# Second matmul of the first MLP: fp32 products replaced by three fp32r products of split halves

## The chip, the cores and the metric

The kernel runs on one core of a Trainium2 chip. The metric is the device time of one execution in microseconds. The kernel before took 510.92 us (median of three runs, 509.15 to 511.65). The core has five engines that run their own instruction queues in program order and meet at semaphores: TensorE (PE, matrix products into PSUM banks), VectorE (DVE), ScalarE (ACT), GpSimd (POOL, no access to PSUM) and SyncE (SP, which issues the DMAs).

## The reference, cut to what matters

One transformer layer on x of shape 8 x 512 x 256. First a block with causal linear attention and an MLP with exact gelu, then a second MLP with ternary weights and a layer norm between its matmuls. The change touches the line marked below.

```python
def attn_block(x, ...):                      # called with _layernorm(x)
    x_norm = _layer_norm(x, ln1_w, ln1_b)
    Q = elu(_linear(x_norm, q_w, q_b)) + 1.0
    K = elu(_linear(x_norm, k_w, k_b)) + 1.0
    V = _linear(x_norm, v_w, v_b)
    attn = _linear(_causal_linear_attn(Q, K, V), o_w, o_b)
    x = x + attn
    h = _layer_norm(x, ln2_w, ln2_b)
    h = gelu(_linear(h, f1_w, f1_b), approximate=False)    # 256 -> 1024
    x = x + _linear(h, f2_w, f2_b)                         # 1024 -> 256: the change
    return x

def ffn(x, ...):                             # called with _layernorm(x)
    h = gelu(x @ absmean(W_fc).T, approximate=False)       # weights -1, 0, 1
    h = layernorm(h, ln_w, ln_b)
    return h @ absmean(W_proj).T
```

## The kernel before, in words

The eight batch elements (g = 0 to 7, 512 rows of 256) are worked one after another, in a software pipeline. `step(g)` holds the first MLP, the second MLP's first half of batch element g, the attention of g + 1, and what is left of g - 1. Each engine has its own lists of calls, `first()`, `step(g)` for g = 1 to 5, and `last()`; the order of the calls in a list is the order of the engine's instructions. There is no scheduler; semaphores alone tie the lists together, and each call begins with the waits it needs.

Precision is kept by splitting. A matrix product in fp32 is either issued as it is, or its operands are cut into a high part (a copy into fp32r, on ACT, the `_hi` calls) and a low part (value less high part, on DVE, the `_lo` calls through `lo_part`, L795), and `split3` (L175 to L179) adds three products in the same bank: high by high, high by low, low by high. Before the change all large products but one went this way. The exception is the second matmul of the first MLP.

The first MLP runs over eight tiles m of 128 hidden columns. `f1(g, m)` writes 128 x 512 into `bank_f[m % 2]` (six products of 512 columns, L177 to L179), `gelu(g, m)` (L581, ACT) reads the bank and writes one tile of `hring`, a ring of `RH` = 8 tiles in SBUF, and `f2(g, k)` (L347) multiplies that tile, as 4 x 128 rows, by `wf2[:, k, :]` and adds it into the two banks `bank_y`: four fp32 products of 128 x 256. f1(m) waits for gelu(m - 2) to free its bank. When f2 is through all eight, `y_sum` (L872, DVE) adds the banks to the residual, a layer norm follows (statistics on DVE, the power on POOL, L1006, the shift on DVE, L773, the scaling on ACT, `z3_norm`), PE flips the result through `bank_f` (`tz3`, L185), and `fc` (L366) starts the second MLP. `tr` (L380) and `proj` (L396), with `g_hi` (L612) and `g_lo` (L912), are its second half; `tu`, `qk_mm`, `scores`, `v_mm`, `attend` and `tz2` belong to attention.

At the start the kernel loads weights and prepares them while batch element 0 goes through attention: `wf1_hi` and `wf1_lo` split the first matmul's weights, `abs_part` (L483) sums the absolute values of the ternary weights, `ternary` (L736, L738) makes them. Small staging tensors (`wqk_raw`, `wv_raw`, `wo_raw`, `wide`, the row selectors) live in the tiles of `hring`, which is not in use yet. On POOL `n1o` (L1024) and `xpb` (L1035) add rows to the residuals.

Of the kernel before, what the change touches and what calls it, by code (L numbers as in the profile page):

```python
# [19 lines left out]
def build(nc, x, wqk_d, wv_d, wo_d, f1_d, f2_d, fc_d, pj_d, vec_d, rows_d, out):  # L20
# [14 lines left out]
    with ExitStack() as ctx:  # L35
# [138 lines left out]
        def _(pe):  # L174
# [227 lines left out]
            def first():  # L402
# [7 lines left out]
                tr(0, 0, 1); tz2(1, 0); fc(0, 3, 0); fc(0, 3, 1); tr(0, 0, 2); proj(0, 0, 0); tr(0, 0, 3)  # L410
                proj(0, 0, 1); tz2(1, 1); tr(0, 1, 0); proj(0, 0, 2); proj(0, 0, 3)

            def step(g):

                f1(g, 0); tr(g - 1, 1, 1); f1(g, 1); tr(g - 1, 1, 2); tu(g + 1, 0); f1(g, 2); f1(g, 3); f1(g, 4)
                tu(g + 1, 1); f1(g, 5); proj(g - 1, 1, 0); tr(g - 1, 1, 3); qk_mm(g + 1); f1(g, 6); f2(g, 0)
                f1(g, 7); f2(g, 1); f2(g, 2); f2(g, 3); scores(g + 1); f2(g, 4); f2(g, 5); f2(g, 6); f2(g, 7)
                v_mm(g + 1, 0); v_mm(g + 1, 1); proj(g - 1, 1, 1); proj(g - 1, 1, 2); proj(g - 1, 1, 3); tz3(g, 0)
                attend(g + 1, 0); attend(g + 1, 1); attend(g + 1, 2); tz3(g, 1); fc(g, 0, 0); attend(g + 1, 3)
                fc(g, 0, 1); fc(g, 1, 0); fc(g, 1, 1); tr(g, 0, 0); tr(g, 0, 1); fc(g, 2, 0); fc(g, 2, 1)  # L420
                tr(g, 0, 2); fc(g, 3, 0); tr(g, 0, 3); proj(g, 0, 0); fc(g, 3, 1); tz2(g + 1, 0); tz2(g + 1, 1)
                proj(g, 0, 1); proj(g, 0, 2); tr(g, 1, 0); proj(g, 0, 3)
# [697 lines left out]
```

## Time and profile before

| | us |
|---|---|
| median of three runs | 510.92 |
| the profiled execution | 510.98 |
| its span | 509.3 |
| PE busy | 479.6 (94%) |
| DVE busy | 349.3 (69%) |
| ACT busy | 289.0 (57%) |
| POOL busy | 129.7 (25%) |
| PE, products of `f2` (L347) | 114.7, 512 records |

The span is the time from the first to the last instruction. Busy is the union of an engine's instructions; PE's ends are modelled, and products overlap in the records, so the pace of products is read from their starts. An idle time is followed by the engine that ended it. In the second fence the granted clock (PEclk) is a share of full speed.

### The profile page before, as it was taken

What the parts mean: (1) busy time and instruction counts of PE and PEld (TensorE: products, weight loads), DVE (VectorE), ACT (ScalarE), POOL (GpSimd) and SP (SyncE); (2) the same over time, 40 slices, a digit from 0 to 9 for tenths busy, and PEclk for the clock granted to TensorE, in tenths of its full rate; (3) what the DMA queues carried; (4) which work ended last, traced back from release to release, by engine and by line L of the source; (5) the groups of instructions that cost most, each with busy time, mean ns of one, the idle gap of its engine ahead of it and who ended that gap; (6) DMA issues with size and microseconds to landing.
All of it is one profiled execution on the core that took longest, in us unless ns stands there. A gap on an engine that the chain in (4) does not pass through costs nothing.

```text
span 509.3 us, 8086 instructions
## 1 busy us (share of the span) xinstructions
PE 479.6 (94%) x2802; PEld 421.8 (83%) x2802; DVE 349.3 (69%) x931; ACT 289.0 (57%) x543; POOL 129.7 (25%) x128
## 2 busy tenths in 40 slices
PE   5786998999999999999999999999999999999796
PEld 4784887888989888888988888888988889888686
DVE  4688528695589638876589639876589638954467
ACT  3654664773557645774557745774559733752263
POOL 2134104220163005420163005420163004302210
PEclk9765999999999999999999999999999999999989
DMA  7230000100010000100010000100010000000001
GB/s 263 99 125 1 1 0 1 42 22 1 1 64 1 21 1 21 44 21 1 1 62 2 22 0 22 42 23 1 0 63 2 21 2 21 2 22 0 22 1 42
DMA packets 10040, 14.03 MB, mean 28 GB/s; under 512 B 784, under 2 KB 9104, under 8 KB 9488
## 3 DMA queue, kind: packets, MB, share of 16 engines
q1 hardware_dynamic: 10000, 13.52, 7.7%
q8 instruction: 22, 0.36, 0.3%
q14 instruction: 18, 0.15, 0.1%
HBM read 9.32 MB, written 4.19 MB: 27 GB/s over the span
## 4 chain that ended last, share of the span: by engine, by line
PE 40%; issue 33%; DVE 10%; POOL 9%; ACT 4%; DMA 2%; SPq 0%; POOLq 0%; DVEq 0%; ACTq 0%
PE bank_y L347 8%; PE bank_f L366 7%; PE bank_p L396 5%; PE bank_f L177 4%; PE bank_f L178 3%; PE bank_f L179 3%; PE bank_y L380 3%; POOL rs L1006 3%; PE bank_a L185 2%; DVE sh L773 2%; DMA out<-yc 2%; POOL y L1042 1%; POOL xa L1024 1%; POOL yc L1052 1%; DVE bn L877 1%
## 5 line engine op out<-in xcount | busy, mean ns | idle before, releaser
L347 PE MATMUL bank_y<-wf,hring 128*128 128x256 f32 x512 | 114.7, 379 | 0.0
L1006 POOL TENSOR_TENSOR rs<-ve,neg_half 128x2 f32<-128x2 f32 x48 | 33.7, 703 | 310.0 <-DVE ve L768 310.0
L347 PEld LDWEIGHTS bank_y<-wf,hring 128*128 128x128 f32 x512 | 96.7, 190 | 13.5
L912 DVE SCALAR_TENSOR_TENSOR g_lo<-bank_y,vec,g_hi 128x256 fp32r<-128x256 f32 x128 | 55.1, 476 | 22.3 <-ACT g_hi L612 22.1
L396 PE MATMUL bank_p<-wpj_t,g_hi 128*128 128x256 f32 x256 | 64.6, 289 | 0.7 <-DVE yc L921 0.7
L581 ACT ACTIVATE hring<-bank_f,f_bias 128x512 f32<-128x512 f32 x64 | 43.2, 686 | 35.1 <-PE bank_f L179 34.5
L396 PE MATMUL bank_p<-wpj_t,g_lo 128*128 128x256 f32 x256 | 62.0, 280 | 0.0
L612 ACT ACTIVATE g_hi<-bank_y,vec 128x256 fp32r<-128x256 f32 x128 | 52.8, 484 | 11.8 <-PE bank_y L380 11.6
L177 PE MATMUL bank_f<-z2T_hi,wf_hi 128*128 128x512 f32 x128 | 55.2, 431 | 1.4 <-DVE z2T_lo L795 1.4
L366 PE MATMUL bank_f<-wfc_t,z3T_hi 128*128 128x512 f32 x128 | 54.3, 424 | 0.9 <-DVE z3T_lo L795 0.9
L603 ACT ACTIVATE h<-bank_f 128x512 f32<-128x512 f32 x64 | 38.7, 604 | 24.1 <-PE bank_f L366 23.9
L178 PE MATMUL bank_f<-z2T_lo,wf_hi 128*128 128x512 f32 x128 | 51.5, 402 | 0.0
L179 PE MATMUL bank_f<-z2T_hi,wf_lo 128*128 128x512 f32 x128 | 51.3, 401 | 0.0
L366 PE MATMUL bank_f<-wfc_t,z3T_lo 128*128 128x512 f32 x128 | 51.2, 400 | 0.0
L396 PEld LDWEIGHTS bank_p<-wpj_t,g_hi 128*128 128x128 f32 x256 | 48.1, 188 | 1.3 <-issue 0.9
L396 PEld LDWEIGHTS bank_p<-wpj_t,g_lo 128*128 128x128 f32 x256 | 48.2, 188 | 0.2
L892 DVE BATCH_NORM_STATS2 bn<-h 128x6 f32<-128x512 f32 x64 | 41.1, 682 | 3.1 <-ACT h L603 2.9
L380 PE MATMUL bank_y<-ident,h 128*128 128x128 f32 x256 | 37.4, 272 | 0.7 <-ACT h L603 0.7
L380 PEld LDWEIGHTS bank_y<-ident,h 128*128 128x128 f32 x256 | 30.7, 141 | 6.1 <-ACT h L603 1.1
L500 ACT ACTIVATE z<-y,sh,rs 128x256 f32<-128x256 f32 x32 | 17.5, 595 | 28.8 <-DVE sh L773 28.8
L773 DVE SCALAR_TENSOR_TENSOR sh<-mv,rs 128x2 f32<-128x2 f32 x48 | 30.4, 634 | 4.0 <-POOL rs L1006 3.5
L366 PEld LDWEIGHTS bank_f<-wfc_t,z3T_hi 128*128 128x128 f32 x128 | 24.6, 192 | 7.8 <-issue 2.3
(156 smaller groups left out, 991.5 us busy)
## 6 DMA issues: line engine op xcount, KB each, us to landing
x_sb<-in_x SPq DMA_DIRECT2D x16, 256.0 KB, 2.8
out<-yc SPq DMA_DIRECT2D x16, 256.0 KB, 2.1
h<-in_f SPq DMA_DIRECT2D x1, 1024.0 KB, 7.6
wf<-in_f SPq DMA_DIRECT2D x1, 1024.0 KB, 9.6
h<-in_fc SPq DMA_DIRECT2D x1, 1024.0 KB, 11.6
h<-in_pj SPq DMA_DIRECT2D x1, 1024.0 KB, 4.9
hring<-in_wv SPq DMA_DIRECT2D x1, 256.0 KB, 3.5
hring<-in_wo SPq DMA_DIRECT2D x1, 256.0 KB, 3.6
```

Source lines behind the costliest of these rows:

```text
L177: pe.matmul(ps, w[0], r[0], start=start, stop=False, skip_group_check=skip)
L178: pe.matmul(ps, w[0], r[1], start=False, stop=False, skip_group_check=skip)
L179: return pe.matmul(ps, w[1], r[0], start=False, stop=stop, skip_group_check=skip)
L347: mm = pe.matmul(bank_y[t // 2][:, (t % 2) * D:(t % 2 + 1) * D], hring[:, (8 * g + k) % RH, t * P:(t + 1) * P], wf2[:, k, :], start=(k == ...
L366: mm = pe.matmul(bank_f[c][:], z3T[part][:, k, t * P:(t + 1) * P], wfc[:, k, c * 512:(c + 1) * 512], start=(k == 0 and part == 0), stop=(k ...
L380: mm = pe.transpose(bank_y[q % 2][:, (2 * i + t) * P:(2 * i + t + 1) * P], h3[:, 2 * h + t, m * P:(m + 1) * P], ident[:])
L396: mm = pe.matmul(bank_p[:, t * D:(t + 1) * D], gr[part][:, (8 * g + 4 * h + q) % RG, i, t * P:(t + 1) * P], wpj[:, m, :], start=(m == 0 an ...
L581: act.activation(hring[:, (8 * g + m) % RH, :], bank_f[m % 2][:], ACT.Gelu, bias=f1_bias[:, m:m + 1]).then_inc(s["h_ready"], 1)
L612: act.activation(gr[0][:, n % RG, i, :], bank_y[q % 2][:, i * D:(i + 1) * D], ACT.Copy, scale=ln3w_c[:, m:m + 1]).then_inc(s["g_hi"], 1)
L892: dve.bn_stats(bn[3][:, t, 6 * c:6 * c + 6], h3[:, t, c * 512:(c + 1) * 512]).then_inc(s["ln4_bn"], 1)
L912: dve.scalar_tensor_tensor(gr[1][:, n % RG, i, :], bank_y[q % 2][:, i * D:(i + 1) * D], ln3w_c[:, m:m + 1], gr[0][:, n % RG, i, :].bitcast ...
L1006: pool.tensor_tensor(rs[n][:, 2 * h:2 * h + 2], ve[n][:, 2 * h:2 * h + 2], neg_half[:, 0:2], ALU.pow).then_inc(s[f"ln{n + 1}_rs"], 1)
```

## The change

- The weights of the second matmul are kept as `wf2_hi` and `wf2_lo` (fp32r). Four ACT copies and four POOL subtractions make them at the start, from raw weights that are loaded into the memory of `y` and `yc`, now one tensor `y_yc`.
- `gelu` writes its result back into `bank_f`. A new ACT call `h_hi` copies the bank into `h_hi`, a new DVE call `h_lo` subtracts that from the bank into `h_lo`. Both are rings of four tiles (`RH` = 4), in place of one ring of eight.
- `f2` calls `split3`: twelve fp32r products of 128 x 256 a tile in place of four fp32 ones. f1(m) and the flips `tz3` now wait for h_lo, not for gelu.
- The staging tensors move from `hring` to `qk_relu`, `z`, `xa` and a small tensor `few_rows`; for this `n1(0)`, `qk_max(0)`, `abs_part(0)` and `xpb(0)` get a wait each.
- The lists of calls of PE, ACT, DVE and POOL are written in another order, in `first`, `step` and `last`.

```diff
-RH = 8
+RH = 4
-        wf2 = sb("wf2", [P, KH, D])
+        wf2 = [sb("wf2_hi", [P, KH, D], F32R), sb("wf2_lo", [P, KH, D], F32R)]
-        hring = sb("hring", [P, RH, N])
+        hr = [sb("h_hi", [P, RH, N], F32R), sb("h_lo", [P, RH, N], F32R)]
...
             def f1(g, m):
...
                 if m >= 2:
-                    pe.wait_ge(s["h_ready"], 8 * g + m - 1)
+                    pe.wait_ge(s["h_lo"], 8 * g + m - 1)
...
             def f2(g, k):
...
-                        pe.wait_ge(s["f2_loaded"], 16)
+                        pe.wait_ge(s["wf2_lo"], 4)
...
-                pe.wait_ge(s["h_ready"], 8 * g + k + 1)
+                pe.wait_ge(s["h_lo"], 8 * g + k + 1)
                 for t in range(T):
-                    mm = pe.matmul(bank_y[t // 2][:, (t % 2) * D:(t % 2 + 1) * D],
-                                   hring[:, (8 * g + k) % RH, t * P:(t + 1) * P], wf2[:, k, :],
-                                   start=(k == 0 and t % 2 == 0), stop=(k == KH - 1), skip_group_check=True)
+                    mm = split3(bank_y[t // 2][:, (t % 2) * D:(t % 2 + 1) * D],
+                                [r[:, (8 * g + k) % RH, t * P:(t + 1) * P] for r in hr], [w[:, k, :] for w in wf2],
+                                k == 0 and t % 2 == 0, k == KH - 1, skip=True)
...
+            def wf2_hi(n):
+                act.wait_ge(s["f2_loaded"], 16)
+                act.activation(wf2[0][:, 2 * n:2 * n + 2, :], f2_raw[:, 2 * n:2 * n + 2, :], ACT.Copy).then_inc(s["wf2_hi"], 1)
...
             def gelu(g, m):
                 act.wait_ge(s["f1_done"], 8 * g + m + 1)
...
+                act.activation(bank_f[m % 2][:], bank_f[m % 2][:], ACT.Gelu, bias=f1_bias[:, m:m + 1]).then_inc(s["h_gelu"], 1)
+
+            def h_hi(g, m):
+                act.wait_ge(s["h_gelu"], 8 * g + m + 1)
                 if 8 * g + m >= RH:
                     act.wait_ge(s["f2_done"], 8 * g + m - RH + 1)
...
+                act.activation(hr[0][:, (8 * g + m) % RH, :], bank_f[m % 2][:], ACT.Copy).then_inc(s["h_hi"], 1)
...
+            def h_lo(g, m):
+                dve.wait_ge(s["h_hi"], 8 * g + m + 1)
+                lo_part(hr[1][:, (8 * g + m) % RH, :], bank_f[m % 2][:], hr[0][:, (8 * g + m) % RH, :], "h_lo")
...
+            def wf2_lo(n):
+                pool.wait_ge(s["wf2_hi"], n + 1)
+                pool.tensor_tensor(wf2[1][:, 2 * n:2 * n + 2, :], f2_raw[:, 2 * n:2 * n + 2, :],
+                                   wf2[0][:, 2 * n:2 * n + 2, :].bitcast(F32), ALU.subtract).then_inc(s["wf2_lo"], 1)
...
PE, def step(g):
-                f1(g, 0); tr(g - 1, 1, 1); f1(g, 1); tr(g - 1, 1, 2); tu(g + 1, 0); f1(g, 2); f1(g, 3); f1(g, 4)
...
+                proj(g - 1, 0, 2); f1(g, 0); f1(g, 1); tu(g + 1, 0); tr(g - 1, 1, 1); proj(g - 1, 0, 3)
+                tr(g - 1, 1, 2); f1(g, 2); proj(g - 1, 1, 0); tr(g - 1, 1, 3); f1(g, 3); f1(g, 4); f2(g, 0)
+                tu(g + 1, 1); f2(g, 1); f1(g, 5); qk_mm(g + 1); f2(g, 2); f1(g, 6); f1(g, 7); f2(g, 3); f2(g, 4)
...
```

On PE, in a middle step, this is the place where the first tile of the second matmul stands. Before, it comes after f1(g, 6), with the last f1 behind it:

```order
L177 MATMUL bank_f<-z2T_hi,wf_hi 128x512
L178 MATMUL bank_f<-z2T_lo,wf_hi 128x512
L179 MATMUL bank_f<-z2T_hi,wf_lo 128x512
L347 MATMUL bank_y<-wf,hring 128x256 x4
L177 MATMUL bank_f<-z2T_hi,wf_hi 128x512
L178 MATMUL bank_f<-z2T_lo,wf_hi 128x512
L179 MATMUL bank_f<-z2T_hi,wf_lo 128x512
```

Now the third tile, f2(g, 2), stands behind the attention's query and key product (`bank_a`); of its twelve products three rows are shown, and f1(g, 6) follows them:

```order
L178 MATMUL bank_a<-uT_hi,wqk_hi 128x512
L179 MATMUL bank_a<-uT_lo,wqk_hi 128x512
L180 MATMUL bank_a<-uT_hi,wqk_lo 128x512
L178 MATMUL bank_y<-wf_hi,h_hi 128x256
L179 MATMUL bank_y<-wf_lo,h_hi 128x256
L180 MATMUL bank_y<-wf_hi,h_lo 128x256
```

The tiles of f2 thus begin right after f1(g, 4) and stand between the later f1; the last five, f2(g, 3) to f2(g, 7), come in one piece, before the scores and not around them.

On DVE, at the start of a middle step (`yc<-bank_p` is `output`, `uT_lo` the split for attention, `qk_relu` the first call behind qk_mm), before:

```order
L904 SCALAR_TENSOR_TENSOR yc<-pj_rows_b,sh,yc 128x256 x2
L921 SCALAR_TENSOR_TENSOR yc<-bank_p,rs,yc 128x256 x2
L795 TENSOR_TENSOR uT_lo<-bank_a,uT_hi 128x2x256
L912 SCALAR_TENSOR_TENSOR g_lo<-bank_y,vec,g_hi 128x256 x2
L795 TENSOR_TENSOR uT_lo<-bank_a,uT_hi 128x2x256
L912 SCALAR_TENSOR_TENSOR g_lo<-bank_y,vec,g_hi 128x256 x4
L806 TENSOR_SCALAR qk_relu<-bank_a,qk_bias 128x512
L892 BN_STATS bn<-h 128x6 x2
```

The same place now:

```order
L933 SCALAR_TENSOR_TENSOR g_lo<-bank_y,vec,g_hi 128x256 x4
L811 TENSOR_TENSOR h_lo<-bank_f,h_hi 128x512
L942 SCALAR_TENSOR_TENSOR y_yc<-bank_p,rs,y_yc 128x256 x2
L933 SCALAR_TENSOR_TENSOR g_lo<-bank_y,vec,g_hi 128x256 x2
L811 TENSOR_TENSOR h_lo<-bank_f,h_hi 128x512
L933 SCALAR_TENSOR_TENSOR g_lo<-bank_y,vec,g_hi 128x256 x2
L811 TENSOR_TENSOR h_lo<-bank_f,h_hi 128x512
L933 SCALAR_TENSOR_TENSOR g_lo<-bank_y,vec,g_hi 128x256 x2
L811 TENSOR_TENSOR h_lo<-bank_f,h_hi 128x512
L811 TENSOR_TENSOR uT_lo<-bank_a,uT_hi 128x2x256
L811 TENSOR_TENSOR h_lo<-bank_f,h_hi 128x512
L811 TENSOR_TENSOR uT_lo<-bank_a,uT_hi 128x2x256
```

The low halves of the new tiles stand one by one between the g_lo of the batch element before, and the two u_lo have moved behind them.

## Rows read from the trace of the kernel before

**Rows 1.** The page's head: span, then busy time of the engines.
```profile
span 509.3 us, 8086 instructions
...
PE 479.6 (94%) x2802; PEld 421.8 (83%) x2802; DVE 349.3 (69%) x931; ACT 289.0 (57%) x543; POOL 129.7 (25%) x128
```
**Rows 2.** Busy by stretch: length, busy (count) of each engine, granted clock, DMA.
```profile
0.00:46.00 46.00, 30.68 (x150) 27.26 (x151) 30.14 (x87) 26.11 (x48) 12.63 (x17) 0.79 0.38 135
...
218.30:275.70 57.40, 56.70 (x344) 50.31 (x344) 41.06 (x112) 34.56 (x66) 15.89 (x15) 1.00 0.06 19
...
460.00:509.30 49.30, 41.10 (x236) 35.55 (x234) 28.71 (x73) 16.32 (x33) 8.46 (x9) 0.95 0.05 17
```
**Rows 3.** Waits of PE from 218.3 to 275.7: in total, times, longest.
```profile
PE bank_f L185 <- ACT z L500: 0.7, 1, 0.7
```
**Rows 4.** Timeline of PE, 230 to 300: start, length, line, out<-in, count.
```profile
243.01 7.07 PE L347 MATMUL bank_y<-wf,hring 128*128 128x256 f32 x32
...
250.03 0.28 PE L178 MATMUL bank_a<-wvo_lo,uT_hi 128*128 128x256 f32 x1
...
252.79 0.28 PE L396 MATMUL bank_p<-wpj_t,g_hi 128*128 128x256 f32 x1
...
255.50 0.28 PE L396 MATMUL bank_p<-wpj_t,g_lo 128*128 128x256 f32 x1
...
276.15 0.39 PE L177 MATMUL bank_f<-z2T_hi,wf_hi 128*128 128x512 f32 x1
...
277.55 0.60 PE L380 MATMUL bank_y<-ident,h 128*128 128x128 f32 x4
```
**Rows 5.** Groups by line and shape: count, busy us, mean ns, idle before.
```profile
L347 PE MATMUL bank_y<-wf,hring 128*128 128x256 f32 x512 | 114.7, 379 | 0.0
...
L581 ACT ACTIVATE hring<-bank_f,f_bias 128x512 f32<-128x512 f32 x64 | 43.2, 686 | 35.1 <-PE bank_f L179 34.5
...
L396 PEld LDWEIGHTS bank_p<-wpj_t,g_hi 128*128 128x128 f32 x256 | 48.1, 188 | 1.3 <-issue 0.9 <-DVE g_lo L912 0.2
...
L795 DVE TENSOR_TENSOR z2T_lo<-bank_a,z2T_hi 128x512 fp32r<-128x512 f32 x16 | 10.9, 689 | 2.3 <-ACT z2T_hi L571 2.3
...
L571 ACT ACTIVATE z2T_hi<-bank_a 128x512 fp32r<-128x512 f32 x16 | 9.5, 596 | 2.9 <-PE bank_a L185 2.9
...
L526 ACT ACTIVATE bank_a<-bank_a,qk_bias 128x512 f32<-128x512 f32 x8 | 5.3, 662 | 2.3 <-DVE qk_relu L806 2.3
```
**Rows 6.** Timeline of ACT, 230 to 300; idle before in brackets.
```profile
243.21 0.38 ACT L552 ACTIVATE af_hi<-bank_a 128x256 fp32r<-128x256 f32 x1 [4.65 <-PE bank_a L274]
...
279.57 0.69 ACT L581 ACTIVATE hring<-bank_f,f_bias 128x512 f32<-128x512 f32 x1 [1.13 <-PE bank_f L179]
280.16 1.56 ACT L612 ACTIVATE g_hi<-bank_y,vec 128x256 fp32r<-128x256 f32 x4
```
**Rows 7.** Timeline of DVE, 230 to 300.
```profile
246.69 0.69 DVE L795 TENSOR_TENSOR ae_lo<-bank_a,ae_hi 128x512 fp32r<-128x512 f32 x1 [6.49 <-ACT ae_hi L546]
```
**Rows 8.** Timeline of PE in the start.
```profile
27.73 0.58 PE L177 MATMUL bank_a<-wvo_hi,uT_hi 128*128 128x256 f32 x1 [1.37 <-DVE ae_lo L795]
...
45.32 0.80 PE L177 MATMUL bank_f<-z2T_hi,wf_hi 128*128 128x512 f32 x1 [1.41 <-DVE z2T_lo L795]
...
50.61 0.39 PE L177 MATMUL bank_f<-z2T_hi,wf_hi 128*128 128x512 f32 x1
```
**Rows 9.** Timeline of POOL in the start.
```profile
26.30 2.95 POOL L1035 TENSOR_TENSOR y<-x_sb,rows_b 128x512 f32<-128x512 f32 x2
37.76 0.71 POOL L1006 TENSOR_TENSOR rs<-ve,neg_half 128x2 f32<-128x2 f32 x1 [8.51 <-DVE ve L768]
```
**Rows 10.** Timeline of DVE in the start.
```profile
22.77 4.11 DVE L711 SCALAR_TENSOR_TENSOR wf_lo<-h,vec,wf_hi 128x512 fp32r<-128x512 f32 x3
...
49.67 0.74 DVE L736 TENSOR_SCALAR yc<-h,theta 128x1024 f32<-128x1024 f32 x1
50.45 1.28 DVE L738 SCALAR_TENSOR_TENSOR wfc_t<-h,theta,yc 128x1024 fp32r<-128x1024 f32 x1
```

More of the change, by code:

```diff
@@ L413, in step @@
+                tz2(1, 0); fc(0, 2, 1); fc(0, 3, 0); proj(0, 0, 0); tr(0, 0, 2); tz2(1, 1); fc(0, 3, 1); tr(0, 0, 3)
+                proj(0, 0, 1); tr(0, 1, 0)
             def step(g):
[L415 to L417 removed]
@@ L418, in step @@
[L418 to L422, printed above, removed]
@@ new lines, in first @@
+                qk_exp(0); wf1_hi(2); qk_hi(0); n1(0); wf1_hi(3); wf2_hi(0); ae_hi(0); af_hi(0); wf2_hi(1); ad_hi(0)
+                wf2_hi(2); eps_split(); v_hi(0, 0); wf2_hi(3); v_hi(0, 1); abs_part(0); abs_part(1); ln3_hi()
+                abs_part(2); abs_part(3); z2_norm(0, 0); z2_norm(0, 1); z2_hi(0, 0); z2_hi(0, 1); u_norm(1, 0)
+                gelu(0, 0); h_hi(0, 0); u_hi(1, 0); gelu(0, 1); h_hi(0, 1); u_norm(1, 1); gelu(0, 2); u_hi(1, 1)
+                h_hi(0, 2); gelu(0, 3); n1(1); h_hi(0, 3); qk_exp(1); gelu(0, 4); h_hi(0, 4); rows(); qk_hi(1)
@@ new lines, in first @@
+                gelu(0, 5); h_hi(0, 5); gelu(0, 6); h_hi(0, 6); ae_hi(1); af_hi(1); ad_hi(1); gelu(0, 7); h_hi(0, 7)
+                spread_copy(); v_hi(1, 0); v_hi(1, 1); z3_norm(0, 0); z3_hi(0, 0); z3_norm(0, 1); z3_hi(0, 1)
+                gelu3(0, 0, 0); gelu3(0, 0, 1); gelu3(0, 1, 0); z2_norm(1, 0); g_hi(0, 0, 0); gelu3(0, 1, 1)
+                gelu3(0, 2, 0); z2_norm(1, 1); g_hi(0, 0, 1); z2_hi(1, 0); gelu3(0, 2, 1); g_hi(0, 0, 2)
+                z2_hi(1, 1); gelu3(0, 3, 0); g_hi(0, 0, 3); gelu3(0, 3, 1); u_norm(2, 0)
@@ L931, in first @@
-                ln2_shift(0, 1); threshold(); z2_lo(0, 0); z2_lo(0, 1); ln1_stats(1); ternary(0); ln1_shift(1)
-                ternary(1); ternary(2); u_lo(1, 0); ternary(3); u_lo(1, 1); qk_max(1); qk_sum(1); qk_lo(1)
-                ad_mask(1); ad_lo(1); ae_lo(1); af_lo(1); y_sum(0, 0); ln3_stats(0, 0); y_sum(0, 1); v_lo(1, 0)
-                ln3_shift(0, 0); v_lo(1, 1); ln3_stats(0, 1); attn_out(1, 0); ln3_shift(0, 1); attn_out(1, 1)
-                ln2_stats(1, 0); attn_out(1, 2); z3_lo(0, 0); z3_lo(0, 1); ln2_stats(1, 1); attn_out(1, 3)
@@ new lines, in first @@
+                consts(); ln1_stats(0); selectors(); ln1_shift(0); wide_cols(); wqk_lo(); u_lo(0, 0); u_lo(0, 1)
+                qk_bias_add(); qk_max(0); bo_rows(); wvo_lo(); qk_sum(0); wf1_lo(0); wf1_lo(1); f1_bias_add()
+                qk_lo(0); wf1_lo(2); ad_mask(0); ae_lo(0); af_lo(0); ad_lo(0); wf1_lo(3); eps_lo(); v_lo(0, 0)
+                v_lo(0, 1); attn_out(0, 0); attn_out(0, 1); ln2_stats(0, 0); attn_out(0, 2); ln2_stats(0, 1)
+                ln2_stats(0, 2); ln2_var(0, 0); attn_out(0, 3); ln2_stats(0, 3); ln2_var(0, 1); ln2_shift(0, 0)
@@ new lines, in first @@
+                ln2_shift(0, 1); ln1_stats(1); z2_lo(0, 0); z2_lo(0, 1); threshold(); ln1_shift(1); ln3_lo()
+                ternary(0); h_lo(0, 0); ternary(1); h_lo(0, 1); u_lo(1, 0); u_lo(1, 1); h_lo(0, 2); ternary(2)
+                qk_max(1); h_lo(0, 3); ternary(3); qk_sum(1); h_lo(0, 4); qk_lo(1); h_lo(0, 5); ad_mask(1); af_lo(1)
+                h_lo(0, 6); h_lo(0, 7); ad_lo(1); ae_lo(1); y_sum(0, 0); ln3_stats(0, 0); y_sum(0, 1); v_lo(1, 0)
+                ln3_shift(0, 0); v_lo(1, 1); ln3_stats(0, 1); attn_out(1, 0); ln3_shift(0, 1); ln2_stats(1, 0)
```

204 lines of the change are left out of this document (102 added, 102 removed).

## The prediction

> **What bounds the kernel now.** I read the page's head first: TensorE (PE) is busy 479.6 of 509.3 us, VectorE (DVE) 69%, ScalarE (ACT) 57% [rows 1]. A mean over stages says little, so next the busy time by stretch [rows 2]. In a middle step (57.4 us, one batch element's MLPs and the next one's attention) PE is busy 56.7 us, DVE 41.1, ACT 34.6. PE idles for 15 us in the first 46 us and for 8 in the last 49. In the middle step the table of waits names one wait of PE, 0.7 us, for the normalised input of the second MLP [rows 3]. So from about 46 to 460 us the time is the sum of what PE is given, and a microsecond taken off PE there is one off the span, as long as DVE and ACT keep up.
>
> The clock was granted at 1.00 in the middle stretches (the 2.4 GHz level), 0.79 in the start [rows 2].
>
> **The products themselves: 19.2 us less.** A tile of the second matmul (`f2`) is four products of 256 columns. In fp32 each leaves two MATMUL records: 64 tiles, 512 records [rows 5]. Their pace is read from start to start, since the durations overlap (a record is 379 ns long): from 243.01, where four tiles begin, to 250.03, where the second product of the next group begins, lie 7.02 us [rows 4]. One fp32r product (0.12, below) is in them, so 32 records take 6.90, 0.216 each. A tile costs 8 x 0.216 = 1.73 us. The new tile is 12 one-record products of 256 columns in fp32r. The kernel has just such work: from 250.03 to 252.79 the value projection runs 23 of them in 2.76 us, 0.120 each, and the last projection 23 in 2.71 from 252.79 to 255.50, 0.118 each [rows 4]. Both load new weights for every product, as the new tile does. I take 0.119: 12 x 0.119 = 1.43 us. Saved: 0.30 us a tile, 64 tiles, 19.2 us (0.118 and 0.120 give 20.1 and 18.6). All tiles lie in stretches where PE is saturated.
>
> A rule that speaks against this is in the Trainium skill, page "TensorE: Matmul & The Clock Gate", section "Part 3: Packing small matmuls": a weight load overlaps matmuls in flight only when it goes to another row group. The trace disagrees here: with loads of 188 ns in front of every product [rows 5] the pace stays 0.119 [rows 4]. I return to it as a rival.
>
> **What ACT and DVE get.** ACT's gelu writes into its bank: the nearest row is the in-place exponential, 662 ns, against 686 for today's gelu into SBUF [rows 5]. Added per tile: one ACT copy bank to fp32r, 0.60 (596 ns), and one DVE subtraction, 0.69 (689 ns) [rows 5]. Per step that is 8 x 0.60 - 8 x 0.02 = 4.6 us on ACT, making 39, and 5.5 us on DVE, making 46.6, in a step of about 54.3: neither is the bound. They also fall in the right half: today in the f1/f2 stage DVE stands idle for 6.49 us and ACT for 4.65 in single waits [rows 6, 7]. No table load comes in between: the `g_hi` copies begin at 280.16, while the gelu of 279.57 (0.69 long) is just ending [rows 6].
>
> **The new waits.** Each bank_f half is now held for gelu, copy and subtraction: 0.66 + 0.60 + 0.69 plus some 0.1 of hops = 2.05 us from the end of f1(m), before f1(m+2) may write it; today 0.7. What PE has queued in between, by the new order, in prices of 1.40 for an f1 (276.15 to 277.55), 0.44 for four transposes (0.60 less 0.16 by which an end is modelled late) [rows 4], 1.43 for an f2 and 0.95 for a proj (8 x 0.119): behind f1(0) 3.7 us, f1(1) 5.0, f1(2) 2.8 (proj, tr, f1(3)), f1(3) 4.7, f1(4) 7.5, f1(5) 4.2. The tightest, f1(2) to f1(4), has 0.75 to spare. Twice something stands in the chain: the two `u_norm` (about 1.1) between gelu(3) and h_hi(3) make 3.1 of 4.7; `qk_max` (about 0.7), which waits for qk_mm, ahead of h_lo(5) makes 3.0 of 4.2. Queued behind a late h_lo on DVE are the g_lo of the batch before and u_lo, for which PE's tr, proj and qk_mm wait. output(g-1,0) stands ahead of h_lo(g,1) and waits for proj(g-1,0,3), which is why that proj is issued before f1(g,2): 2.4 us are left there. The ring of four asks only that f2(m-4) is done before h_hi(m); by the new order f2(3) ends before gelu(7) can start. Unforeseen stalls are bounded by 0 and, by the larger of the two chain links (0.69) once per step in 7 steps, 5 us; I take 0.5, near zero since every slack found is above 0.7.
>
> The 0.7 us wait in front of the second z flip [rows 3] stands in five middle steps. Behind the last f2 PE has 6.2 us of work ahead of the first flip (scores, two proj, v_mm, proj) where it had 5.7, and 2.8 instead of 2.9 between the flips. Bounds: nothing, and all 3.3 us gone; I take 1.6.
>
> **The start.** DVE now does two wf1_lo (1.37 each [rows 10]) and the bias before qk_lo, so scores(0) begins about 1.0 us later; but ae_lo no longer stands behind three wf1_lo, so v_mm(0), today at 27.73 [rows 8], moves by about 0.5 only. On POOL four wf2_lo (nearest row 1.5 each, the adds of that shape [rows 9]) come before xpb(0); the last waits for an ACT copy at about 32, so xpb(0) ends near 36.5, and ln2_rstd(0,0) is wanted at 37.76 [rows 9]: hidden, by 1.2 us. The four ACT copies (0.7 each) fill waits. wqk_hi behind u_norm(0) is hidden too: its low part is first read by qk_mm(0). Start: +0.5, bounds -0.5 and +2. In the first batch element the four ternary() (0.74 + 1.28 = 2.0 each on DVE [rows 10]) alternate with h_lo; f1(0,2) then waits for a subtraction that ends near 50.8 where it started at 50.61 today [rows 8]. +0.8, bounds 0 and +3.
>
> **Sum**, against the profiled execution's own 510.98 (span 509.3 and 1.7 around it; the median of the three runs is 510.92, the same): 510.98 - 19.2 - 1.6 + 0.5 + 0.5 + 0.8 = 492.0 us.
>
> **Rivals.**
> *The helpers bind in part.* h_lo comes late behind another DVE instruction in some tiles, PE stays the bound in the rest. For it: both queues are in order, every f1 now waits on two engines. Against it: 16 us of DVE idle per step today, 5.5 used. At 0.12 us a tile (7.7 us) the time is 500.
> *The chain replaces the saving (the slower side).* If the bank hand-over exposes one whole subtraction, 0.69 us, on every tile because h_lo always queues behind a g_lo that waits for ACT, 64 x 0.69 = 44 us are added: 536. The point from which it decides is 0.30 us a tile (2.4 us a step): beyond it the change loses. Against it: the slacks above are all larger than 0.7.
> *Weight loads show.* If the four more loads of a tile (12 for 8) were not hidden, 4 x 0.19 = 0.75 us a tile, 48 us: 540. Against it: the pace in rows 4. This is what the Trainium skill's rule on weight loads ("TensorE: Matmul & The Clock Gate", "Part 3") would make of it.
> *The start swallows it.* If wf2_lo delayed the z2 chain, at most 4 x 1.5 = 6 us: 498. Against it: the 1.2 us of slack.
>
> **Chances.** Forecast case 0.78 (own range 488 to 496), helpers in part 0.10, start 0.03, chain 0.07, weight loads 0.02. Low end: 510.98 - 20.1 - 3.3 - 0.5 + 0 = 487. High end: +2 and +3 at the start and 5 of stalls above 491.8 give 500, about which the partial rival lies; above it is left some 0.15. So 487.5 to 500. Half a per cent (2.6 us) is about what a measurement of this kernel can tell. Faster needs under 508.4: forecast, partial and start rival, 0.91, less a little for a chain that costs about what is gained: 0.90; same 0.03; slower 0.07.
>
> **What would show it.** In the changed trace: L178 to L180 writing bank_y, 768 records at 0.119 from start to start (wrong at 0.15 or more: the saving is gone at 0.144); a middle step of 54.3 to 54.7 us with PE idle under 1; waits of PE on DVE's h_lo under 0.5 us a step; DVE near 46.5 and ACT near 39 us a step; f1(0,0) within 1 us of today's 45.32 [rows 8]. The prediction is wrong if PE's waits on h_lo add up to more than 5 us, or PE's records are not faster.

## The result, and the profile after

The changed kernel takes 489.36 us (median of 4 runs, 487.23 to 490.18), the kernel before in the same comparison 510.13 (4 runs, 509.15 to 511.65): ratio 0.959, 95% interval 0.955 to 0.963. The forecast was 492.0, range 487.5 to 500. The profiled execution took 487.23, of which 485.5 are the span. Two executions further down lay far outside their fellows and are left out of every median here: one of 573.11 us (gelu in SBUF, new order) and the profiled one of 2513.73 us in experiment 4, so that the version with two more subtractions has no usable trace.

The page's head after, against [rows 1]: TensorE (PE) is busy for less time, the three helpers (DVE, ACT, POOL) for more.

```profile
span 485.5 us, 8738 instructions
...
PE 455.8 (94%) x3058; PEld 413.8 (85%) x3058; DVE 379.1 (78%) x995; ACT 326.1 (67%) x611; POOL 135.3 (28%) x132
```

The start, a middle step (f1(4,0) to f1(5,0)) and the end by stretch, against [rows 2]: length, busy (count) of PE, PEld, DVE, ACT, POOL, granted clock, DMA.

```profile
0.00:43.60 43.60, 27.16 (x148) 24.26 (x148) 29.12 (x91) 26.58 (x51) 19.18 (x22) 0.85 0.41 142
...
207.47:261.42 53.95, 53.93 (x376) 49.68 (x375) 44.33 (x119) 39.08 (x74) 15.96 (x16) 1.00 0.06 21
460.00:485.50 25.50, 21.49 (x130) 18.30 (x128) 17.86 (x46) 11.78 (x25) 1.79 (x3) 0.90 0.06 21
```

PE idles 0.02 us of 53.95: PE's work fills the middle step, and the step is 3.5 us shorter.

Groups by line and shape, against [rows 5]: the new products, one of the three groups of their weight loads, the subtraction, the gelu and the copy.

```profile
L178 PE MATMUL bank_y<-wf_hi,h_hi 128*128 128x256 f32 x256 | 72.1, 282 | 1.0 <-DVE h_lo L811 1.0
L179 PE MATMUL bank_y<-wf_lo,h_hi 128*128 128x256 f32 x256 | 71.5, 279 | 0.0
L180 PE MATMUL bank_y<-wf_hi,h_lo 128*128 128x256 f32 x256 | 71.4, 279 | 0.0
...
L180 PEld LDWEIGHTS bank_y<-wf_hi,h_lo 128*128 128x128 f32 x256 | 48.0, 187 | 0.0
...
L811 DVE TENSOR_TENSOR h_lo<-bank_f,h_hi 128x512 fp32r<-128x512 f32 x64 | 43.9, 688 | 28.3 <-ACT h_hi L593 27.5
L587 ACT ACTIVATE bank_f<-bank_f,f_bias 128x512 f32<-128x512 f32 x64 | 42.2, 660 | 13.9 <-PE bank_f L180 12.3
L593 ACT ACTIVATE h_hi<-bank_f 128x512 fp32r<-128x512 f32 x64 | 38.1, 597 | 3.3 <-PE bank_y L180 1.7
```

768 records, as foreseen, and in all of them only 1.0 us of waiting. A record's 280 ns is a duration; the pace is read from start to start. Timeline of PE in a dense stretch, first and last row shown (columns: start, length, line, out<-in, count):

```profile
232.10 0.28 PE L180 MATMUL bank_y<-wf_hi,h_lo 128*128 128x256 f32 x1
...
235.28 0.28 PE L180 MATMUL bank_y<-wf_hi,h_lo 128*128 128x256 f32 x1
```

27 products lie between the two starts: 3.18 / 27 = 0.118 us each, the pace of [rows 4].

Where the time went, from the starts of f1(g,0) in both traces: start -1.7 us; the first two steps together -5.9 (the new order moves two `proj` from the first into the second, so they are taken together); four middle steps -3.54 each, -14.2; from f1(6,0) to the end -2.0. Together -23.8; by medians -20.8, since the execution profiled after was the fastest of its four and the one profiled before lay 0.85 above the median of its four.

### The profile page after: what moved, and what is told of

Read it like the earlier page. It is cut to its first block, busy times and chain, and to the rows that moved or that the text cites. A ratio compares the mean times of both kernels' runs of the same rounds, so it can differ in the third digit from the quotient of the medians.

```text
span 485.5 us, 8738 instructions
## 1 busy us (share of the span) xinstructions
PE 455.8 (94%) x3058; PEld 413.8 (85%) x3058; DVE 379.1 (78%) x995; ACT 326.1 (67%) x611; POOL 135.3 (28%) x132
## 4 chain that ended last, share of the span: by engine, by line
PE 69%; DVE 12%; issue 10%; POOL 3%; ACT 3%; DMA 0%; DVEq 0%; POOLq 0%; ACTq 0%
PE bank_f L367 9%; PE bank_p L397 9%; PE bank_y L178 6%; PE bank_y L179 5%; PE bank_y L180 5%; PE bank_f L178 5%; PE bank_f L179 5%; PE bank_f L180 5%; PE bank_y L381 4%; PE bank_a L178 3%; PE bank_a L180 3%; PE bank_a L179 3%; PE bank_a L186 2%; DVE sh L789 2%; DVE g_lo L933 2%
## 5 line engine op out<-in xcount | busy, mean ns | idle before, releaser
L178 PE MATMUL bank_y<-wf_hi,h_hi 128*128 128x256 f32 x256 | 72.1, 282 | 1.0 <-DVE h_lo L811 1.0
L179 PE MATMUL bank_y<-wf_lo,h_hi 128*128 128x256 f32 x256 | 71.5, 279 | 0.0
L180 PE MATMUL bank_y<-wf_hi,h_lo 128*128 128x256 f32 x256 | 71.4, 279 | 0.0
L811 DVE TENSOR_TENSOR h_lo<-bank_f,h_hi 128x512 fp32r<-128x512 f32 x64 | 43.9, 688 | 28.3 <-ACT h_hi L593 27.5
L178 PE MATMUL bank_f<-z2T_hi,wf_hi 128*128 128x512 f32 x128 | 52.7, 412 | 1.4 <-DVE z2T_lo L811 1.4
L587 ACT ACTIVATE bank_f<-bank_f,f_bias 128x512 f32<-128x512 f32 x64 | 42.2, 660 | 13.9 <-PE bank_f L180 12.3
L180 PE MATMUL bank_f<-z2T_hi,wf_lo 128*128 128x512 f32 x128 | 51.1, 399 | 0.0
L178 PEld LDWEIGHTS bank_y<-wf_hi,h_hi 128*128 128x128 f32 x256 | 48.1, 188 | 2.7 <-DVE h_lo L811 1.2
L179 PEld LDWEIGHTS bank_y<-wf_lo,h_hi 128*128 128x128 f32 x256 | 48.0, 188 | 1.1
L180 PEld LDWEIGHTS bank_y<-wf_hi,h_lo 128*128 128x128 f32 x256 | 48.0, 187 | 0.0
L1054 POOL TENSOR_TENSOR xa<-xa,bo_b 128x512 f32<-128x512 f32 x16 | 21.4, 1359 | 93.0 <-ACT xa L507 93.0
```

Of the source, the lines that this page charges most:

```text
L178: pe.matmul(ps, w[0], r[0], start=start, stop=False, skip_group_check=skip)
L179: pe.matmul(ps, w[0], r[1], start=False, stop=False, skip_group_check=skip)
L180: return pe.matmul(ps, w[1], r[0], start=False, stop=stop, skip_group_check=skip)
L587: act.activation(bank_f[m % 2][:], bank_f[m % 2][:], ACT.Gelu, bias=f1_bias[:, m:m + 1]).then_inc(s["h_gelu"], 1)
L811: dve.tensor_tensor(dst, b, hi.bitcast(F32), ALU.subtract).then_inc(s[ready], 1)
L1054: pool.tensor_tensor(half(xa, h), half(xa, h), wide_row(bo_b[:]), ALU.add).then_inc(s["n1o_ready"], 1)
```

## The experiments

The kernel before ran beside each group on the same chip (medians 510.73, 511.07, 510.09). The changed kernel was rerun only in the first group (experiments 1, 2 and 3, and the two waits of 8); where a version of another group is set against its 488.31, the difference is one between chips, on which the kernel before differs by up to 1.0 us. "Step" below is the distance between two middle f1(g,0): 57.4 us before, 53.9 after.

**1. The changed kernel again**, to tell its own spread from effects.

> The changed kernel once more, unaltered, as the measure for the runs beside it. The profiled execution of it took 487.2 us while the others took 488.7 to 490.2, so this also tells which is typical. Expected: 489.4, plus or minus 1.5. Theory 'start': f1(0, 0) begins at 43.6 us again, 1.7 before the kernel before, because wf1_lo on DVE no longer runs beside POOL's adds. Rival 'luck': the start was a chance of one execution and f1(0, 0) lies anywhere between 43.6 and 46.

Measured: 488.31 (5 runs, 487.51 to 489.53), ratio 0.956 (0.954 to 0.958). Steps are the same to 0.02 us. f1(0,0) stood at 45.0, not 43.6, so most of the 1.7 us that the first trace shows at the start was chance; over nine traces of kernels in the new order it stood at 43.6 to 45.6, mean 44.5. In the one trace of before it stood at 45.3, and in the three other traces with the old lists (experiments 5 and 7) at 44.5 to 45.0. A gain at the start is therefore not shown.

**2. fp32 products in the new order**: the tables of the change, with the old second matmul, weights and ring, and no halves.

```diff
-    mm = split3(bank_y[...], [r[:, (8 * g + k) % RH, ...] for r in hr], [w[:, k, :] for w in wf2], ...)
+    mm = pe.matmul(bank_y[...], hring[:, (8 * g + k) % RH, ...], wf2[:, k, :], ...)
...
-    act.activation(bank_f[m % 2][:], bank_f[m % 2][:], ACT.Gelu, ...)
+    act.activation(hring[:, (8 * g + m) % RH, :], bank_f[m % 2][:], ACT.Gelu, ...)
```

> The new lists of calls and the moved staging memory, but the second matmul as before: fp32 products, gelu straight into a ring of eight, no copy, no subtraction, no split of its weights. Theory 'products': what is left of the change is the order and the start, worth 1.7 us at the start and about 0.7 us a middle step of waits, so 510.1 - 1.7 - 3.5 = 505, and the products account for 64 x (1.72 - 1.43) = 18.6 of the rest less the helpers' share. Rival 'order': the new order carries much of the gain, and this kernel comes in under 500.

Measured: 508.02 (506.96 to 508.23), ratio 0.994 (0.992 to 0.996), step 56.4. That is 3 us above the 505 expected, which had counted the 1.7 us of the start as real, and far above the rival's 500. So the order, with the moved staging memory, is worth 2.7 us alone, and products with their helpers 508.02 - 488.31 = 19.7 us (19.2 forecast), 2.5 a step. PE waits for `z` at the z flips: before 7.6 us in 9 places, here 4.1 in 3.

```profile
PE bank_f L186 <- ACT z L504: 4.1, 3, 2.2
PE bank_y L381 <- DVE g_lo L928: 3.7, 4, 1.7
```

The second row is new with the order, not with the halves: two of its waits are 1.63 and 1.66 us long. The middle step from f1(3,0) to f1(4,0), in the columns of [rows 2]:

```profile
216.50:272.90 56.40, 56.37 (x344) 50.45 (x343) 39.24 (x111) 34.74 (x66) 15.90 (x16) 1.00 0.06 20
```

DVE is busy 39.2 us of it, where it was 41.1 before: the new order alone takes 1.9 us off DVE.

**3. Two products in place of three** (the weights' low half left out of the second matmul).

```diff
-    mm = split3(...)          # hi*hi, hi*lo, lo*hi
+    pe.matmul(ps, hr[0][...], wf2[0][:, k, :], ...)
+    mm = pe.matmul(ps, hr[1][...], wf2[0][:, k, :], ...)
```

> The changed kernel with the product of the high half of h and the low half of wf2 left out, so two products in place of three; all copies and subtractions stay. 256 products of 0.119 us go, 30.5 us of PE. Theory 'PE is the only bound, with slack beside it': the time falls by 25 to 30 us, to 460 to 464, with a middle step of 50.1. Rival 'the helpers are just behind PE': DVE at 44.7 and ACT at 39.4 us of a 53.9 us step, and the hand-over of a bank (2.05 us) against only 2.8 us of PE work, let PE wait; the time falls by less than 15 us.

Measured: 473.7 (471.0 to 475.98, two executions near each end), ratio 0.927 (0.922 to 0.932), step 51.9. 256 products at 0.119 are 30.5 us; 14.6 came, and 2.0 of 3.8 in a middle step. The expected 460 to 464 was missed and the rival came out: the helpers are just behind PE. PE's waits:

```profile
PE bank_y L349 <- DVE h_lo L813: 10.8, 7, 2.8
```

In each middle step this is one wait of 1.5 us, before the last tile of the second matmul. Timeline of ACT before it (idle in brackets):

```profile
220.72 1.28 ACT L589 ACT_TABLE_LOAD   x1
222.01 0.66 ACT L589 ACTIVATE bank_f<-bank_f,f_bias 128x512 f32<-128x512 f32 x1
222.71 0.60 ACT L595 ACTIVATE h_hi<-bank_f 128x512 fp32r<-128x512 f32 x1
223.20 0.58 ACT L543 ACTIVATE q_stack<-bank_a 64x512 fp32r<-64x512 f32 x1
...
225.74 0.60 ACT L595 ACTIVATE h_hi<-bank_f 128x512 fp32r<-128x512 f32 x1
```

ACT runs nearly without a gap through a table load (`ACT_TABLE_LOAD`, 1.28 us, here back to gelu after the exponential) and the q and k copies, and h_hi of the last tile ends at 226.3. The changed kernel is therefore close to the end of this lever: with 3.8 us less work on PE in a step, the helpers already take half of it back.

**4. One and two more subtractions on DVE ahead of each h_lo.**

```diff
     dve.wait_ge(s["h_hi"], 8 * g + m + 1)
+    dve.tensor_tensor(spare[:, 0, ...], bank_f[m % 2][:], hr[0][...].bitcast(F32), ALU.subtract)
     lo_part(hr[1][...], bank_f[m % 2][:], hr[0][...], "h_lo")
```

> The changed kernel with one more DVE subtraction over 128 x 512 ahead of each h_lo, out of the same two tiles into spare memory (0.69 us each by h_lo's own row, 64 of them: 44 us of DVE in all). Theory (TensorE is the bound of a step, the wait for h_lo has slack, my bank chain's was 2.05 us): in a middle step DVE's work goes from 44.7 to 50.2 of 53.9 us and stays under it; the last row of products of a tile comes after h_lo by at least 0.7 us nearly everywhere, so the five middle steps stay at 53.9 to 54.4 and the whole kernel loses 0 to 3 us (most of it in the tail, where DVE ends the pass): 488 to 491. Rival (chain: f1 - gelu - h_hi - h_lo - f2 binds, no slack): each tile pays its 0.69 us, steps of 59.4 and a kernel of 525 to 532.

> The same with two more subtractions (1.38 us per tile). Theory: DVE's work in a middle step comes to 44.7 + 11.0 = 55.7 us, more than the 53.9 us of TensorE, so DVE becomes the bound: a middle step takes at least 55.8, with TensorE's waits for DVE some 2 to 5 us a step, and the kernel 500 to 520. If the slack were only that of the average (DVE free to run ahead), steps would be 55.7 to 56.5 (kernel 500 to 506); if the slack of the single tile (2.05 us) is the limit too, the waits in the dense stretch of f2 come on top (kernel 506 to 520). Rival (no slack at all): 64 times 1.38, a kernel of 570 or more.

Measured: with one 499.43 (498.49 to 500.34), ratio 0.978 (0.975 to 0.981); with two 520.7 (three executions, 519.3 to 520.9). A middle step with one:

```profile
265.22:319.71 54.49, 54.16 (x376) 49.55 (x375) 48.80 (x127) 38.99 (x74) 15.93 (x16) 1.00 0.07 20
```

Its waits of PE have two rows of this kind, f2 for its tile and f1 for its bank:

```profile
PE bank_y L179 <- DVE h_lo L812: 2.8, 1, 2.8
...
PE bank_f L179 <- DVE h_lo L812: 2.1, 6, 0.5
```

Eight subtractions more (DVE busy 48.8 us where it was 44.3) cost 0.6 us there, a little over the 0.5 that the forecast allowed: the slack of a middle step is real and holds most of one subtraction, but not all. In each of the five middle steps f1(g,4) now waits 0.3 us for the h_lo that frees its bank; this is the link that the prediction called the tightest. The kernel lost 11.1 us, not 0 to 3, since the two steps at the ends hold no slack (against the repeat of experiment 1 the step from f1(6,0) is 4.2 us longer, of which the first row, a wait for h_lo(6,7), is the most; the tail 2.4; the first two steps 1.9; the four middle ones together 2.3). With two subtractions the loss is 32.4 us, just above the 506 to 520 that the bound by DVE's sum and the single tile's slack gave.

**5. The halves in the old order** (the tables of before, each h_lo placed by hand, ring of eight), then **the same with gelu in SBUF**, so that the bank is free after gelu; and **gelu in SBUF in the new order**.

```diff
-    f1(g, 0); f1(g, 1); tu(g + 1, 0); tr(g - 1, 1, 1); proj(g - 1, 0, 3); tr(g - 1, 1, 2); f1(g, 2)
+    f1(g, 0); tr(g - 1, 1, 1); f1(g, 1); tr(g - 1, 1, 2); tu(g + 1, 0); f1(g, 2); f1(g, 3); f1(g, 4)
... and, in the two with gelu in SBUF:
-    pe.wait_ge(s["h_lo"], 8 * g + m - 1)      # f1: bank free
+    pe.wait_ge(s["h_gelu"], 8 * g + m - 1)
-    act.activation(bank_f[m % 2][:], bank_f[m % 2][:], ACT.Gelu, ...)
+    act.activation(hf[:, (8 * g + m) % 3, :], bank_f[m % 2][:], ACT.Gelu, ...)
```

> The changed products, gelu and halves, in the order of the kernel before on every engine: each high half follows its gelu at once, each h_lo stands on DVE among the old entries just ahead of where f2 needs it, the ring has eight tiles. It asks how much of the gain needs the new order. Theory: the order alone was worth 1.0 us a step with fp32 products; with halves the old order also puts two f2 close behind their f1 (f1(g,6), f2(g,0), f1(g,7), f2(g,1) to f2(g,7)), and the work of DVE and ACT around them was placed for a kernel without halves, so I expect TensorE to wait 0.5 to 2 us a step for h_lo or gelu and for what the halves delay: middle steps of 55.0 to 56.5, kernel 496 to 506. Rival (the order matters little, products carry all): steps of 54.5 to 54.9, kernel 491 to 494. Other rival (helpers unplaced eat the gain): steps of 57.4 and more, kernel at 510 or above.

> The old order with gelu in an SBUF ring of three tiles, the bank free after gelu. It asks why the old order with the halves took 60.8 us a step (530.7 in all). Theory (the bank chain: f1(m + 2) waited for h_lo(m), 16.8 us in 16 places by the waits, because the bank is now held until h_lo and the old order puts f1(m + 2) close behind f1(m)): these waits go and steps fall by 3 to 5 us to 56 to 58, kernel 500 to 512. Rival (it is the added work of ACT and DVE in the wrong places, whatever the bank): steps stay at 60 or more, kernel 525 to 531.

> The changed kernel, but gelu writes to an SBUF ring of three fp32 tiles, from which ACT's copy and DVE's subtraction read; the bank of f1 is free after gelu, as in the kernel before, and no longer held until h_lo. It asks what keeping gelu in its bank costs or gives. Theory of my bank chain (2.05 us of slack, so holding the bank costs nothing in the new order; SBUF operands cost DVE something beside POOL only): middle steps 53.8 to 54.2, kernel 487.5 to 490.5; h_lo's mean row goes from 0.69 to 0.72 to 0.85 where POOL works beside it. Rival (holding the bank costs): steps of 53.0 to 53.6 and 484 to 487. Other rival (reads from SBUF slow DVE for good): h_lo 1.0 and more, kernel 491 to 496.

Measured: old order 530.74 (529.49 to 531.51), ratio 1.039 (1.036 to 1.041), step 60.8: slower than before, where I had expected 496 to 506. This is the second rival of that expectation. Its waits of PE:

```profile
PE bank_f L178 <- DVE h_lo L806: 16.8, 16, 4.8
PE bank_f L186 <- ACT z L507: 15.3, 15, 2.1
PE bank_y L178 <- DVE h_lo L806: 4.9, 5, 1.0
```

The first row is f1, not f2: it waits for its bank. The place in one step, on DVE and then on PE:

```profile
291.22 1.24 DVE L784 SCALAR_TENSOR_TENSOR sh<-mv,rs 128x2 f32<-128x2 f32 x1
292.49 1.87 DVE L920 SCALAR_TENSOR_TENSOR y_yc<-pj_rows_b,sh,y_yc 128x256 f32<-128x256 f32 x2
294.28 0.86 DVE L937 SCALAR_TENSOR_TENSOR y_yc<-bank_p,rs,y_yc 128x256 f32<-128x256 f32 x2
295.07 1.27 DVE L806 TENSOR_TENSOR h_lo<-bank_f,h_hi 128x512 fp32r<-128x512 f32 x2
```

```profile
295.80 0.50 PE L178 MATMUL bank_f<-z2T_hi,wf_hi 128*128 128x512 f32 x1 [1.62 <-DVE h_lo L806]
```

f1(m+2) stands close behind f1(m), and h_lo(m) behind the corrections and the output of the batch before: in these lists I had put the first four h_lo of a step there. Another place for them in the old lists was not tried. The bank hand-over of the rival "the chain replaces the saving" is thus real, only in another order. Freeing the bank after gelu took 14.8 us off: 515.97 (515.23 to 516.72), ratio 1.010 (1.007 to 1.013), step 59.6, and no wait of f1 for h_lo is left in it; but it is still slower than before, with 16.0 us of waits for `z` (15 places), 6.1 for k_lo and 5.2 of f2 for h_lo, none of which the bank touches. Of the 14.8 us a middle step has only 1.2; the first two steps have 6.5. So the theory of the bank was half of it: my 56 to 58 a step was missed, and so were the rival's 525 to 531. How much of the rest is my placing stays open. In the new order gelu in SBUF gave 490.19 (three executions, 488.62 to 490.45), ratio 0.959 (0.956 to 0.962), same steps of 53.9: there the held bank costs nothing, and h_lo's mean is 690 ns in SBUF too.

**6. The ring of eight in the new order.**

```diff
-RH = 4
+RH = 8
```

> The changed kernel with rings of eight tiles in place of four. Theory (the ring of four holds nobody up: h_hi(m) needs f2(m - 4), which TensorE has long issued in the order of the lists): middle steps 53.8 to 54.0 and a kernel within 1 us of the changed one (487.5 to 489.5). Rival (the memory saved costs waits: h_hi waits for f2_done, 2.2 us in three places by the waits of a middle stretch): 0.1 to 0.5 us a step, 1 to 4 us in all, so 484 to 487.

Measured: 488.46 (487.64 to 489.67), ratio 0.957 (0.954 to 0.959), steps 53.9: the ring of four holds nobody up.

**7. POOL held back in the kernel before.**

```diff
 def n1o(g):
+    pool.wait_ge(s["wf1_lo"], 4)      # for g == 0
```

> The kernel before with one edit: POOL's n1o(0) waits until the four wf1_lo of DVE have run. It asks why wf1_lo took 1.37 us each before (three, ending at 26.88) and 0.70 after. Theory (the two engines get in each other's way when both read their operands from SBUF: POOL's n1o ran at 23.23 to 26.33 and xpb at 26.30 to 29.25): with POOL held back wf1_lo takes 0.69 to 0.75 each, ends some 2 us sooner, and the row of n1o(0) falls from 3.10 to under 2.6; f1(0,0) starts 0 to 2 us sooner if wf1_lo was on its path, later by up to 1 us if xpb(0) now ends last; kernel 508 to 511. Rival (wf1_lo is slow for what it reads, for instance a weight tile that a transfer is still filling): 1.3 us each as before, POOL or not.

Measured: 510.0 (10 runs, 508.51 to 511.05), ratio 0.998 (0.997 to 1.000), f1(0,0) 0.85 us sooner. The three wf1_lo of [rows 10], 4.11 us with POOL's adds beside them, and POOL's n1o:

```profile
22.80 2.08 DVE L711 SCALAR_TENSOR_TENSOR wf_lo<-h,vec,wf_hi 128x512 fp32r<-128x512 f32 x3
```

```profile
28.93 2.70 POOL L1025 TENSOR_TENSOR xa<-xa,bo_b 128x512 f32<-128x512 f32 x2 [21.48 <-DVE wf_lo L711]
```

0.69 each instead of 1.37, with the same data: it is POOL. Its own pair falls from 3.10 to 2.70 (under 2.6 was expected). The 0.85 us at f1(0,0) are within the scatter of experiment 1.

**8. Two waits, then three, taken out of the changed kernel**, by moving DVE's `correct` of the batch before behind what PE waits for.

```diff
-    ... ln1_shift(2); correct(0, 0)                       # first element
+    ... ln1_shift(2); g_lo(0, 0, 3); correct(0, 0)
-    h_lo(6, 6); ln4_stats(5, 3); ln4_var(5, 1); correct(5, 1)      # last step
+    h_lo(6, 6); ln4_stats(5, 3); ln4_var(5, 1)                     # correct(5, 1) now ahead of output(5, 1)
-    z2_lo(7, 1); correct(6, 0); g_lo(6, 0, 2)             # the third
+    z2_lo(7, 1); g_lo(6, 0, 2)                            # correct(6, 0) now ahead of output(6, 0)
```

> The changed kernel with two orders on DVE altered: g_lo(0, 0, 3) stands ahead of correct(0, 0) at the seam of first() and step(1), and correct(5, 1) stands right ahead of output(5, 1), no longer ahead of h_lo(6, 7). In the changed kernel's trace PE waits 1.63 us for the first and 1.03 for the second, both behind corrections that take 1.9 us in place of 0.9 while POOL adds. Theory 'PE is the bound': both waits go, the time falls by 2 to 2.7 us against the unaltered kernel beside it. Rival 'another wait is behind them': under 1 us.

> The version with two waits taken out, and the third too: DVE's correct(6, 0) goes from ahead of g_lo(6, 0, 2) to just ahead of output(6, 0), since tr(6, 1, 1) waited 1.65 us for g_lo at 427 us. Theory: that wait goes, with nothing new in its place, 1.2 to 1.7 us off the two-wait version's 487.44: 485.5 to 486.5. Rival (as with the second wait of the two-wait version, the time comes back later in the last stretch, where DVE sets the pace and the granted clock drops after each wait): 487 to 488.

Measured: two waits out, 487.44 (485.66 to 488.41), ratio 0.954 (0.951 to 0.956): in the trace the first wait fell from 1.63 to 0.25 us and the second is gone, and f1(7,0) came 2.5 us sooner than in the repeat. But the median gained only 0.9, as the rival had it. In that trace the stretch from f1(7,0) to the end was 1.7 us longer than in the repeat, with a granted clock of 0.91 from 422 to 440; in the repeat and in the trace after the result the same wait stands at that place and the clock there was 1.00. Why it fell once stays open. Three waits out: 484.57 (483.96 to 486.24), ratio 0.949 (0.947 to 0.952), the best version here and a little under the 485.5 to 486.5 expected. It lies 3.7 us under the changed kernel, 3.4 by the two ratios. Of PE's waits for g_lo, 3.7 us in the changed kernel, this is left, and no row for h_lo:

```profile
PE bank_y L381 <- DVE g_lo L933: 0.5, 2, 0.3
```

## Why the prediction was right, and where it was off

*The products (-19.2).* Right in place and size: pace 0.118, count 768, and 19.7 us by experiment 2, the helpers' cost and the one wait for h_lo (1.0 us) already in it. In a middle step it is 2.5 us, where 8 x 0.30 = 2.4 was forecast.

*Weight loads.* They did not show. The loads' group L180 stands at 187 ns each with no idle time, beside products paced at 0.118. The Trainium skill's rule ("TensorE: Matmul & The Clock Gate", "Part 3: Packing small matmuls") that a load overlaps only with another row group is not borne out here. The same section also lets a load be pulled ahead when it goes to a background weight buffer; no run here shows which buffer a load took.

*Helpers.* DVE took 44.3 us of a step where 46.5 were forecast, ACT 39.1 (39). DVE's miss is in the old work, not in the new: with the new order alone it was busy 39.2 us and not 41.1 (experiment 2), and the halves added 5.1 (5.5 forecast). In the old order one of the two `correct` of a middle step ran beside POOL's adds and took 1.87 us, in the new one both take 0.88. Experiment 4 shows that a middle step has room for most of one more subtraction per tile; that it has none for two follows only from the kernel's time. No wait for h_lo in the middle steps, as forecast.

*The bank chain (2.05 us, slack from 0.75 up).* Right in that nothing waits in a middle step, and right about the tightest link, f1(2) to f1(4). The slack there was over-stated: one more subtraction of 0.69 us made f1(4) wait 0.3 us (experiment 4), which leaves some 0.4 of the 0.75. The slacks were read from the new order, and experiment 5 shows that they hang on it: with the halves in the old lists, as I placed them, the kernel loses 20 us on before instead of gaining 22. How much of that a better placing in the old lists would win back was not tried, so the order's own share of the gain is known only with fp32 products (2.7 us).

*The z flip (-1.6).* Under-sized. I took half; the 0.7 us wait went whole in every middle step, and the order gave 1.0 a step in all (57.4 to 56.4), the remainder in many small gaps between groups. My step of 54.3 was 53.9.

*The start and first element (+0.5, +0.8).* No delay of the start shows: nine traces in the new order have f1(0,0) at 44.5 in the mean, 0.8 before the one trace of before. They scatter by 2.0 us, so the sign of the term stays open; the first trace, at 43.6, lay outside the 1 us that the prediction allowed. One price in it was wrong: I had put two wf1_lo in front of qk_lo at 1.37 each, from [rows 10]. That row was taken beside POOL's adds; in the new order the two run at 18.76, before these adds start at 21.82. Timeline of DVE after:

```profile
18.76 1.39 DVE L727 SCALAR_TENSOR_TENSOR wf_lo<-h,vec,wf_hi 128x512 fp32r<-128x512 f32 x2
...
22.17 1.47 DVE L727 SCALAR_TENSOR_TENSOR wf_lo<-h,vec,wf_hi 128x512 fp32r<-128x512 f32 x1
```

0.70 each alone, 1.47 with POOL: the duration I took was that of a collision, and experiment 7 shows it. The ternaries between the h_lo cost nothing: PE has no wait for h_lo in that element.

*Unforeseen stalls (+0.5).* This is the term that was most under-sized: three stalls, 4.3 us. Timeline of PE:

```profile
103.04 0.63 PE L381 MATMUL bank_y<-ident,h 128*128 128x128 f32 x4 [1.63 <-DVE g_lo L933]
...
399.59 0.38 PE L178 MATMUL bank_y<-wf_hi,h_hi 128*128 128x256 f32 x1 [1.03 <-DVE h_lo L811]
...
427.55 0.63 PE L381 MATMUL bank_y<-ident,h 128*128 128x128 f32 x4 [1.65 <-DVE g_lo L933]
```

And DVE ahead of them. POOL adds beside all three; its row beside the third is shown:

```profile
100.24 1.86 DVE L925 SCALAR_TENSOR_TENSOR y_yc<-pj_rows_b,sh,y_yc 128x256 f32<-128x256 f32 x2
...
396.13 1.88 DVE L925 SCALAR_TENSOR_TENSOR y_yc<-pj_rows_b,sh,y_yc 128x256 f32<-128x256 f32 x2
...
423.71 2.91 DVE L925 SCALAR_TENSOR_TENSOR y_yc<-pj_rows_b,sh,y_yc 128x256 f32<-128x256 f32 x2
```

```profile
424.88 2.87 POOL L1073 TENSOR_TENSOR y_yc<-y_yc,xa 128x512 f32<-128x512 f32 x2
```

Each time `correct` stands ahead of the half that PE needs. Moving it took 3.4 to 3.7 us off (experiment 8). I had looked for trouble only in the chain of the h tiles, all of whose links my slacks covered, and not in the lists of the first and last step, where two of the three waits come with the order alone (experiment 2).

*The sum.* By medians of one comparison (510.73, 508.02, 488.31) products and helpers gave -19.7 for -19.2, order and start together -2.7 for the +0.2 of my four small terms. In the traces of before and of experiment 2 this is -0.5 at the start, -0.7 in the first two steps, -4.1 in the four middle steps and +2.3 from f1(6,0) to the end: -3.0. One new wait for g_lo of 1.6 us stands in the first two steps and one in the last stretch. The forecast fall was 19.0 us: 3.4 too small against that comparison (22.4), 1.8 against the first (20.8). So the small terms missed both ways and partly cancelled: the flips and the gaps gave more than I took, and the stalls in the first and last step cost 3.8 us more. That much of the near hit is luck.

*The range.* Its ends do not follow from their own sums. The low sum is 487.1 and the range starts at 487.5; the high sum, 491.8 with 2, 3 and 5, is 501.8 and not 500. Neither decides anything here.

## What to carry to other kernels

When a helper's result must come back before a buffer is free, the order of the lists can decide whether the change gains or loses: count what the bounding engine has queued between two users of the buffer, in the first and last pass too and not only in the steady one. A duration taken from a row is that of its neighbourhood; before it goes into a sum, see what POOL did beside it. Once the bounding engine is gapless, further cuts on it may pay only in part (half, in experiment 3).
